# Local attention in a two-layer decoder: keys scaled on the scalar engine, and another order of work where one batch follows another

## The reference

```python
q = (x @ Wq.T)...; k = (x @ Wk.T)...; v = (x @ Wv.T)...     # x is layer-normed
q = _rms_norm(q, qn_w); k = _rms_norm(k, kn_w)
q = q * cos + _rotate_half(q) * sin
k = k * cos + _rotate_half(k) * sin
scores = einsum(q, k) * Dh ** (-0.5), masked to 0 <= i - j <= 64
out = softmax(scores) @ v
x = x + out @ Wo.T
```

## Time and profile before

| | |
|---|---|
| median of 3 runs | 1400.53 us (1397.14 to 1403.43) |
| profiled execution | 1384.34 us, span 1382.5 us |
| PE, PEld busy | 1214.4 us (88%), 940.9 us (68%) |
| DVE, ACT, POOL busy | 957.8 us (69%), 760.1 us (55%), 606.2 us (44%) |
| granted clock of TensorE, mean | 0.949 |
| local attention, scores of the first unit to the end of the stage | about 585 to 1047 us of the span |

### The profile page before, as it was taken

The page is one execution under the profiler, slowest core; times in us unless marked ns, Lnnn a source line. Parts: engine busy times, 40 slices in busy tenths (PEclk is TensorE's granted clock), DMA queues, the critical chain, the costliest instruction groups (busy, mean ns, idle before and its releaser), DMA issues. The chain is left out here.

```text
span 1382.5 us, 24786 instructions
## 1 busy us (share of the span) xinstructions
PE 1214.4 (88%) x7679; PEld 940.9 (68%) x7726; DVE 957.8 (69%) x1855; ACT 760.1 (55%) x1757; POOL 606.2 (44%) x745
## 2 busy tenths in 40 slices
PE   6895899989989985489998999989987999969998
PEld 5673444558888874367777777777774666648887
DVE  5999799856755458877777777777764767744443
ACT  5433477763555454566666666666662666633332
POOL 2000556552164454776666666676663343310000
PEclk9998899989999998699999999999997999989999
DMA  9001000010035314200000000000000000000000
GB/s 335 3 1 53 15 16 16 12 62 1 9 98 155 104 50 168 110 1 1 2 0 0 0 0 0 0 0 0 1 1 5 4 4 3 2 1 1 16 15 32
DMA packets 27422, 44.74 MB, mean 32 GB/s; under 512 B 5648, under 2 KB 22160, under 8 KB 25936
## 3 DMA queue, kind: packets, MB, share of 16 engines
q1 hardware_dynamic: 23888, 34.31, 7.2%
q0 software_dynamic: 3456, 9.44, 2.6%
HBM read 32.21 MB, written 9.44 MB: 30 GB/s over the span
## 5 line engine op out<-in xcount | busy, mean ns | idle before, releaser
L2334 ACT ACTIVATE wi_weights<-wi_psum,wi_bias,wi_scale 128x128 f32<-128x128 f32 x256 | 113.7, 454 | 120.2 <-DVE wi_bias L2454 120.2
L2109 POOL TENSOR_TENSOR wi_straight<-wi_straight,wi_crossed 128x512 f32<-128x512 f32 x80 | 103.0, 1288 | 10.9 <-DVE wi_crossed L2440 10.8
L978 DVE TENSOR_REDUCE gq_least<-gq_psum 128x4 f32<-128x512 f32 x128 | 84.6, 685 | 15.5 <-PE gq_psum L861 13.8
L2097 POOL TENSOR_TENSOR wi_scratch<-wi_sums,wi_eps 128x4 f32<-128x4 f32 x80 | 33.8, 422 | 129.8 <-DVE wi_sums L2413 128.4
L2098 POOL TENSOR_TENSOR wi_scale<-wi_scratch,minus_half 128x4 f32<-128x4 f32 x80 | 84.5, 1057 | 6.3
L2224 PE MATMUL wi_psum<-wi_k_t,wi_q_t 128*128 128x128 f32 x512 | 68.0, 276 | 20.8 <-ACT wi_q_t L2325 19.5
L940 ACT ACTIVATE gq_weights_t<-gq_psum 128x512 f32<-128x512 f32 x128 | 67.7, 601 | 23.4 <-PE gq_psum L881 23.1
L2175 PEld LDWEIGHTS wi_psum<-const,wi_straight 128*128 128x128 f32 x320 | 39.1, 142 | 54.6 <-issue 36.1
L2445 DVE TENSOR_REDUCE wi_top<-wi_psum 128x4 f32<-128x512 f32 x64 | 43.8, 684 | 45.8 <-PE wi_psum L2224 45.8
L2427 DVE TENSOR_TENSOR wi_straight<-wi_raw,rows 128x512 f32<-128x512 f32 x80 | 71.6, 895 | 0.0
L2119 POOL TENSOR_TENSOR wi_weights<-wi_weights,wi_inverse 128x512 f32<-128x512 f32 x64 | 66.4, 1038 | 9.5 <-remote 5.1
(11 more groups left out here) (410 smaller groups left out, 3780.3 us busy)
## 6 DMA issues: line engine op xcount, KB each, us to landing
slot_y<-ex_s_out SPq DMA_DIRECT2D x20, 256.0 KB, 2.2
x<-in_x_dram SPq DMA_DIRECT2D x4, 512.0 KB, 8.1
gate<-in_gate_dram SPq DMA_DIRECT2D x2, 1024.0 KB, 6.6
up<-in_up_dram SPq DMA_DIRECT2D x2, 1024.0 KB, 8.6
down<-in_down_dram SPq DMA_DIRECT2D x2, 1024.0 KB, 10.5
egu<-in_egu_dram SPq DMA_DIRECT2D x1, 2048.0 KB, 15.5
gq_keys_diagonal<-gq_key_parts SPq DMA_DIRECT2D x64, 32.0 KB, 1.9
wo<-in_wo_dram SPq DMA_DIRECT2D x1, 2048.0 KB, 8.8
```

The source lines that it names most:

```text
L978: dve.tensor_reduce(least[:, n // 2 % 2, n % 2, j, :], ps[:, j % 2, :].rearrange("p (v t) -> p v t", t=P), AX.X, ALU.min).then_inc(topped, 1)
L2109: added_up = pool.tensor_tensor(straight[:, at], straight[:, at], crossed[:, at], ALU.add)
L2334: act.activation(weights[:, g % 2, j, :], ps[:, SC + g % 2, j * P:j * P + P], ACT.Exp, bias=bias[:, g % 2, j:j + 1], scale=scale[:, g, j:j ...
```

## The change

- Keys. POOL's second instruction of `join` goes. A new ACT step, `scale_keys`, multiplies the keys in place by their scale, with four activations of 128x128 (one for each head, with the scale as a column). `turn_heads` of the keys waits for these. `find_scale` of the keys now signals through a semaphore of its own.
- ACT, unit 3: `scale_keys` and `take_turned` of the keys stand before `weigh(t, 3)`, where `take_turned` stood behind it.
- PE: keys are transposed before `attend(t, 2)`, not behind it. The third queries of the next batch are projected in unit 3, between `attend(t, 2)` and the transposes of the first queries, and no more in unit 0. In `scores` the mask's matmul no longer waits for the transposed queries; the four that follow do. The wait for `k_t` is gone (the wait for `q_t` covers it).
- DVE, unit 3: `maximum` and `shift` of unit 3 stand before `rotate_crossed` of q0. `rotate` is cut in two, `add_squares` and `rotate_straight`, and `invert(t, 3)` stands between them.
- POOL, unit 3: `normalise(t, 3)` stands before `find_scale` of q1.

```diff
@@ POOL
                 if what == "k":
+                    need(pool, keys_scaled, 4 * t)
+                else:
+                    pool.wait_ge(keys_scale, t + 1)
...
-                added_up = pool.tensor_tensor(straight[:, at], straight[:, at], crossed[:, at], ALU.add)
-                if what == "k":
-                    link(added_up)
-                    added_up = pool.tensor_tensor(straight[:, at], straight[:, at],
-                                                  wide(scale[:, scale_at], [P, 4, DH]), ALU.mult)
-                added_up.then_inc(rotated, 1)
+                pool.tensor_tensor(straight[:, at], straight[:, at], crossed[:, at], ALU.add).then_inc(rotated, 1)
...
+                    if g == 3:
+                        normalise(t, g)
                     for item in items[:1]:
                         find_scale(*item)
-                    normalise(t, g)
+                    if g < 3:
+                        normalise(t, g)
@@ PE
-                if g == 0:
-                    pe.wait_ge(turned_taken, number("k", t) + 1)
-                pe.wait_ge(turned_taken, number("q", t, g) + 1)
...
+                pe.wait_ge(turned_taken, number("q", t, g) + 1)
                 for j in range(4):
...
-                        if item[0] != "v":
+                        if item[0] != "v" and g > 0:
                             project(*item)
...
+                    if g == 3 and not last:
+                        turn_heads("k", t + 1, 0)
                     if g > 0 or not first:
                         attend(*earlier(t, s, g, 1, U))
                     if g < 3:
                         turn_heads("q", t, g + 1)
                     elif not last:
-                        turn_heads("k", t + 1, 0)
+                        project("q", t + 1, 1 - s, 2)
                         turn_heads("q", t + 1, 0)
@@ ACT
+            def scale_keys(t):
+                act.wait_ge(keys_scale, t + 1)
+                act.wait_ge(rotated, of_five("k", t, 0) + 1)
+                for j in range(4):
+                    act.activation(straight[:, K, j, :], straight[:, K, j, :], ACT.Copy,
+                                   scale=scale[:, 4, j:j + 1]).then_inc(keys_scaled, 1)
...
+                    if g == 3 and not last:
+                        scale_keys(t + 1)
+                        take_turned("k", t + 1, 1 - s)
                     weigh(t, g)
                     if g == 3 and not last:
-                        take_turned("k", t + 1, 1 - s)
                         take_turned("q", t + 1, 1 - s, 0)
@@ DVE
                         take_weights(t, 2)
-                        if not last:
-                            rotate_crossed("q", t + 1, 1 - s, 0)
                     maximum(t, g)
...
                     shift(t, g)
...
+                    if g == 3 and not last:
+                        rotate_crossed("q", t + 1, 1 - s, 0)
                     for item in items[:1]:
-                        rotate(*item)
+                        add_squares(*item)
+                    if g == 3:
+                        invert(t, g)
+                    for item in items[:1]:
+                        rotate_straight(*item)
                         rotate_crossed(*item)
-                    invert(t, g)
+                    if g < 3:
+                        invert(t, g)
```

34 lines of the change are left out of this document (22 added, 12 removed).

## The result

Five runs of each on one chip: 1381.13 us with the change (1376.45 to 1386.71) against 1399.11 before (1395.65 to 1403.43), a ratio of 0.9877, 95% interval 0.984 to 0.9914, which is 12 to 22 us. The forecast was 1389 us, 11 us faster, in a range of 1377 to 1403.

What follows compares the result with a forecast made beforehand. The prediction took PE's order of work to bound the kernel. 15 turns by 0.7 us, 10.5 us, or 11 or so with the first batch, brought 1400.5 to 1389.5 (forecast 1389), own range 1385 to 1394, over all cases 1377 to 1403.

Steps and rivals of the forecast that it cites:

- the term per turn: Local attention, each of 15 turns: 0.6 us at `attend(t, 3)` plus 0.1 for unit 1's scores, 0.7 us gained.
- Keys: Four ACT activations scale the keys behind POOL's join, taking 1.3 us, so the keys are ready at 840.5.
- Shift of unit 3: On DVE, with POOL idle, this shift costs 0.15 us and ends at 841.1, not 842.61.
- The collision: POOL's `normalise(t, 3)` gets into DVE's crossed pair of q1, costing it 1.03 us; the layer norm still beats q1's join.
- A DVE instruction that starts inside a 128x512 instruction of POOL waits for its end: Rule read from the earlier trace for DVE beside POOL: q0's shift takes 0.73 us where the next takes 0.15.
- The other 0.1 us: Scores of unit 1 no longer wait in front of their mask, 0.1 us more gained per turn.
- PE's order of work sets the time: PE is busy 388.88 of 422.85 us, so gains must come from its gaps, 2.45 us per turn.
- no more scores waiting for `q_t` for 1.2 us: Sign of being right: the waits of PE's scores for transposed queries, 16 before, 19.5 us in all, disappear.
- First and last batch: In the first batch, q2 ahead of q0's transposes and ACT's key scaling cost what they save, 0 within 1 us.
- Rival 1: No collision of POOL's `normalise` with DVE's crossed pair: 1.2 to 1.35 us gained per turn, 1381 us; chance 0.25.
- Rival 2: DVE's layer norm falls behind q1's join: 0.45 us lost per turn, 1407 us; chance 0.13 in full, 0.12 half its turns.
- Rival 3: Nothing gained, 1400 us: slow keys on ACT, PE stalls, late `weigh`, or DVE and GpSimd SBUF instructions excluding each other; chance 0.15.

Runs made afterwards that it cites:

- e4: Changed kernel with DVE's crossed part of q0 again ahead of the maximum and shift of unit 3: 1387.55 us, ratio 0.9929.
- e2: Changed kernel with the third queries projected in unit 0 again: 1382.33 us, ratio 0.9887.
- e8: Changed kernel with PE's order and waits as before the change, the other engines keeping their new order: 1391.75 us, ratio 0.9977.
- e1: Changed kernel with DVE's inversion of unit 3 again behind q1's straight and crossed parts: 1381.52 us, ratio 0.989.
- e7: Changed kernel with POOL's join of q1 directly behind the normalising of unit 3, ahead of q1's scale: 1389.45 us in one run.
- e10: Kernel before the change with only DVE's maximum and shift of unit 3 moved ahead of q0's crossed pair: 1400.65 us, ratio 1.0011.
- e9: Changed kernel with inversion behind q1's pair, POOL's join of q1 ahead of its scale, and DVE's layer norm behind unit 0's shift: 1380.86 us, ratio 0.9849.

## Why the prediction was right, and where it was not

The forecast's path is what happened, from the keys on ACT over the unblocked shift and the stretched pair to a layer norm that wins against the join. The size of the term per turn was off: 0.95 us where it had 0.7. By its steps, on the clock of before:

- **Keys.** 1.28 us against 1.3, queued right behind the join (0.09). The Trainium skill, ScalarE: Activation LUTs, section "What ACT_TABLE_LOAD costs", gives 186 ns and 0.833 ns an element for an activation, 93 ns more for a column operand, and neighbours that overlap by 93 ns. By estimate from these figures that is 386 ns each and 1.26 us for four. The 64 of the changed kernel show a mean of 391 ns, so the trace agrees.
- **Shift of unit 3** 0.16 (0.15 foretold; e4 prices it, 0.58 us), **`weigh`** at 841.70 (841.7), **queries by keys** at 844.62 (844.8).
- **The collision.** The pair lasted 1.63 us (1.75 foretold), and the layer norm won against the join by 0.3 us (0.1 to 0.3). The detail is another: POOL wasn't let in with the pair in mid-way, its `normalise` started 0.02 us ahead of it. Only in the first two turns and in the last does `normalise` get in between the two halves, and the pair lasts about the same there (1.60).
- **"A DVE instruction that starts inside a 128x512 instruction of POOL waits for its end"** was too wide. Those that read PSUM don't wait: in the same turn of before `take_weights` starts at 839.65, inside POOL's L2112, and takes 0.68 us. The sum didn't use it for them.
- **Where the size came from.** The pair ended at 845.93 and not 846.1, the layer norm started at 846.46 and not 846.7, `attend` at 848.11 and not 848.35. DVE's chain was counted too long by small amounts, 0.24 us in all, and this is the term that was mis-sized: 0.87 us at `attend` where it had 0.63. The other 0.1 us, for the scores of unit 1 that no longer wait ahead of their mask, is right on average: 0.02 us in one turn, 0.16 in the next.
- **"PE's order of work sets the time"** was half the reading of the earlier trace rows. It holds from `attend(t, 3)` on, where the turn takes the same 17.1 us in nearly every kernel. Ahead of it the turn goes by POOL's `normalise` and by DVE's `split_out` and `take_weights`, and the gap of 0.94 us that the projection of q2 filled is worth nothing (e2). The sum came out near because it followed DVE to `attend` and didn't add up the gaps. What PE's order does bring is the keys before `attend` (e8), since the exponentials stand behind `k_t` on ACT.
- **The sign "no more scores waiting for `q_t` for 1.2 us"** came true only in its number. The wait is still there behind the mask, 0.55 us on PE's row (0.94 by the load) where PE's row had 1.27. The prediction's own times (mask behind transposes that end at 843.9, queries at 844.8) contained it.
- **First and last batch.** What lies ahead of the first unit 0 was counted at 0 within 1 us and gained 0.2. The last batch was not counted and lost 2.1. Of this 0.8 lies ahead of the scores of unit 3, where the shift of unit 0 fell into the join and lasted 0.70 us, not 0.15:

```profile
1016.04 1.29 POOL L2111 TENSOR_TENSOR wi_straight<-wi_straight,wi_crossed 128x512 f32<-128x512 f32 x1
1016.64 0.70 DVE L2472 SCALAR_TENSOR_TENSOR wi_bias<-wi_top,wi_scale 128x4 f32<-128x4 f32 x1
...
1038.34 0.98 PEld L2246 LDWEIGHTS wi_psum<-wi_wo_high,wi_out_high 128*128 128x128 f32 x4
```

  The other 1.3 lies behind them. There the granted clock is at the lower level (1.2 GHz) for 3.4 us, and the four loads of `project_out` take 0.98 instead of 0.54 us; the profile before shows no such stretch there. It doesn't go with the change: the idle time of PE ahead of it is 3.34 us in all 14 profiles, and e1, e2, e4 and e7 have no such stretch (12.5 us from unit 3's queries by keys to the end, as the 12.6 of before), while the others, e10 among them, have it (13.7 to 14.1 us).
- **Rival 1** (no collision, 1.2 us or more) is e1: the pair went unstretched and the gain did not come. Its size came in e9, 1.32 us under before, where the shift and the layer norm are out of the join's way too. **Rival 2** is e7 in a milder form, since the join starts sooner there: 0.56 us a turn back, and still 0.4 under before; slower than before was not seen. **Rival 3's** rule, which the prediction quotes from the Trainium skill, SBUF — State Buffer, section "Who interferes with whom", does not hold for POOL's 128x4 power: its L2104 runs from 845.69 to 846.70, and DVE's straight part, begun in it at 846.08, takes 0.69 us, its time alone.
- **The chances** add up with a slip: the cases named as within 0.5% make 0.32 with the 0.02 of rival 2, not 0.30.
- **The whole.** Local attention's 12.7 us is near the 11 foretold. The median fell by 18.0, and 12.7 is inside its interval. The other 5 us are not shown to belong to the change: experts vary by 20 us and cross attention by 5 with the same code. So 1381 lies in the stated range, but outside the forecast's own 1385 to 1394, and that it is rival 1's number is luck: rival 1's course is not what happened.
